# Between the two layers of a graph network kernel: another order, and rooms of their own, for the last three tiles

## What is computed

```
# layer 0
mean = segment_sum(x[src], dst) / max(degree, 1)      # x itself where the degree is 0
x1   = layernorm(x + relu(concat(x, mean) @ W.T + b))
# layer 1: Q, K, V by node type, keys turned by the edge's type
score = sum(Q[dst] * (K[src] @ W_edge[etype])) / sqrt(128) * mu[etype]
out   = segment_sum(softmax_by_dst(score) * V[src])
y     = layernorm(x1 + out)
```

## Time and profile before

| | us |
|---|---|
| median of 3 runs | 2977.58 (2977.36 to 2982.68) |
| the profiled execution | 2978.1 |
| its span, first to last instruction | 2976.3 |
| around the span | 1.8 |
| layer 0, its last gather issued | 928.5 |
| POOL idle between the layers | 928.5 to 969.4 |
| layer 1, from its first gather | 972.9 to 2976.3 |

### The profile page before, as it was taken

How to read it: one execution, slowest core, us unless ns; L and a number is a source line. 1 busy time by engine, 2 the same in 40 slices (tenths; PEclk the granted TensorE clock), 3 DMA queues, 4 the chain that set the end, 5 groups by cost and what they waited for, 6 DMA issues and landing times.

```text
span 2976.3 us, 39076 instructions
## 1 busy us (share of the span) xinstructions
PE 2377.8 (80%) x13828; PEld 1832.4 (62%) x13828; DVE 1543.9 (52%) x5341; ACT 1152.8 (39%) x2071; POOL 2205.6 (74%) x2291
## 2 busy tenths in 40 slices
PE   4999999999998678777777767767767867777776
PEld 2677777777776456556556555655655655655655
DVE  7899999999996233333333333333333333333334
ACT  6565556656564232223233232233222323322223
POOL 7777777777773777777777777777777777777774
PEclk7999999999999688888888888888888888888888
DMA  7355555565554444344444444444434444434442
GB/s 194 104 163 170 160 162 162 162 175 170 164 161 151 119 116 115 112 116 116 114 116 116 112 116 117 115 114 116 115 113 116 116 114 116 116 112 116 115 114 70
DMA packets 256965, 384.07 MB, mean 129 GB/s; under 512 B 100640, under 2 KB 189003, under 8 KB 250625
## 3 DMA queue, kind: packets, MB, share of 16 engines
q0 software_dynamic: 108112, 273.13, 33.1%
q1 hardware_dynamic: 146833, 107.53, 11.7%
q10 hardware_dynamic: 1824, 0.92, 0.1%
HBM read 304.30 MB, written 77.13 MB: 128 GB/s over the span
## 4 chain that ended last, share of the span: by engine, by line
POOL 72%; issue 23%; PE 3%; DMA 1%; DVE 1%; ACT 0%; POOLq 0%; ACTq 0%; DVEq 0%; SPq 0%
POOL ring L722 50%; POOL ring L717 14%; POOL spare_n L717 7%; POOL ring L692 1%; PE banks L789 1%; DMA ring<-in_x_dram 0%; PE banks L1041 0%; PE banks L862 0%; PE banks L1004 0%; PE banks L815 0%; PE banks L867 0%; PE banks L1033 0%; DMA ring<-x_part_rows,work 0%; PE banks L874 0%; DMA x_part_rows<-sums 0%
## 5 line engine op out<-in xcount | busy, mean ns | idle before, releaser
L722 POOL DMA_INDIRECT ring<-kv_table,src_n x1563 | 1495.2, 957 | 476.1 <-issue 476.1
L1017 PE MATMUL banks<-identf,ring 128*128 128x128 f32 x1568 | 293.3, 349 | 505.6 <-DMA ring<-kv_table,src_n 504.4
L1724 DVE COPY sums<-banks 128x512 f32<-128x512 f32 x392 | 260.0, 688 | 738.1 <-PE banks L1033 736.6
L789 PE MATMUL banks<-sums,picks 128*126 128x385 bf16 x2401 | 581.8, 327 | 0.0
L1017 PEld LDWEIGHTS banks<-identf,ring 128*128 128x128 f32 x1568 | 242.2, 182 | 528.6 <-DMA ring<-kv_table,src_n 527.1
L1180 ACT ACTIVATE picks<-banks 128x343 bf16<-128x343 f32 x882 | 433.4, 512 | 317.4 <-PE banks L781 308.5
L717 POOL DMA_INDIRECT ring<-x_part_rows,work x462 | 450.9, 976 | 141.6 <-issue 140.5
L1261 ACT ACTIVATE work<-banks,negmax 128x2048 f32<-128x2048 f32 x98 | 192.8, 1967 | 789.6 <-DVE negmax L1670 775.9
L1269 ACT ACTIVATE work<-banks 128x512 f32<-128x512 f32 x392 | 223.0, 596 | 591.6 <-PE banks L1017 578.4
L1667 DVE TENSOR_REDUCE largest<-banks 128x1 f32<-128x2048 f32 x98 | 224.6, 2292 | 358.4 <-PE banks L1004 358.4
L789 PEld LDWEIGHTS banks<-sums,picks 128*126 128x126 bf16 x2401 | 323.6, 137 | 110.3 <-issue 25.0
(11 more groups left out here) (256 smaller groups left out, 2279.4 us busy)
## 6 DMA issues: line engine op xcount, KB each, us to landing
kv_table<-ring SPq DMA_DIRECT2D x48, 1024.0 KB, 4.1
ring<-kv_table,src_n POOLq DMA_INDIRECT x1563
sums<-x_typed SPq DMA_DIRECT2D x99, 128.0 KB
x_typed<-work SPq DMA_DIRECT2D x49, 256.0 KB
ring<-x_part_rows,work POOLq DMA_INDIRECT x462
x_part_rows<-sums SPq DMA_DIRECT2D x7, 675.5 KB, 5.0
spare_n<-x_part_rows,work POOLq DMA_INDIRECT x224
sums<-x_rows SPq DMA_DIRECT2D x51, 64.0 KB, 3.1
```

The costliest lines, as they stand in the source:

```text
L722: pool.indirect_dma_start(kv_ring[u][:, j, :], None, table, bass.IndirectOffsetOnAxis(ap=of, axis=0)).then_inc(l1_rows[2 * u + j // RUN], 16)
L789: mm = pe.matmul(bank[2 + i % 2][0:SLOTS, 0:3 * D + 1], picked[:, i % 2, h, 0:SLOTS], x_parts[:, h, 0:3 * D + 1], start=(h == 0), stop=(h ...
L1017: tr = pe.transpose(bank[KEY_BANK[g]][:, j * P:(j + 1) * P], kv_ring[k.u][:, g * 4 + j, 0:D], identf[:, :])
L1724: dve.tensor_copy(prob[:, g * 4:(g + 1) * 4, :].rearrange("p a b -> p (a b)"), bank[PROB_BANK[g]]).then_inc(prob_copied, 1)
```

## The change

The last three tiles are called `third` (46), `before` (47) and `last` (48).

- Tile 46's first half is done at the beginning of step 48 (h = 4, 11, 15 in place of 30, 36, 42), in bank 1, and its x1 is turned at h = 34. Tile 47's x and mean are turned at h = 36 and 47, in bank 3. ACT and DVE have an order of their own for this step (`last_step`).
- After the step PE's order interleaves the second halves of the three tiles with the first halves of 47 and 48, as written out below; ACT's and DVE's orders go with it.
- Rooms: the table rows of tile 47 go to `kv_before` and the typed rows of tile 48 to `typed_last`, both in the half of `picks` that step 48 doesn't use. Products of keys go to bank 1 for tile 47 and bank 2 for tile 48, values of tile 48 and the last node sum to bank 4. The turned x1 of all three goes to the fourth quarter of its front bank instead of bank 6.
- Waits are moved with it: those that guarded the shared banks go or move to `low_keys` and `high_keys`, `project_values` of tiles 46 and 47 waits for the copy of the values before (bank 5), and `by_types` of tile 48 no longer waits for the typed rows of tile 47 to be stored.

The diff, cut to its core (left out are the replaced names in the two stores of SP, in `transpose_mean` and `add_nodes`, and the removed PE functions `finish_and_begin` and `late_part`):

```diff
@@ -207,6 +207,9 @@
 near = [t.bitcast(BF16).rearrange("p (j c) -> p j c", c=TW) for t in near_runs]
+late_part = parts(picks, [TILES * P // 2], TILES * P)
+kv_before = late_part(ET * 2 * D).rearrange("p (e c) -> p e c", c=2 * D)
+typed_last = by_type(late_part(NT * D))
@@ -439,10 +442,13 @@
 def kv_of(tile):
-    return kv_last if tile.t == TILES - 1 else kv_rows
+    return {TILES - 1: kv_last, TILES - 2: kv_before}.get(tile.t, kv_rows)
+
+def typed_of(tile):
+    return typed_last if tile.t == TILES - 1 else x1_typedT
...
 def wait_row(e, tile):
-    if 0 < tile.t < TILES - 1:
+    if 0 < tile.t < TILES - 2:
@@ -454,10 +460,24 @@
-FRONT_BANK = {TILES - 1: 0, TILES - 2: 4}
+FRONT_BANK = {TILES - 1: 0, TILES - 2: 3, TILES - 3: 1}
+KEY_PRODUCT = {TILES - 1: 2, TILES - 2: 1}
+VALUE_PRODUCT = {TILES - 1: 4}
...
     return bank[FRONT_BANK[tile.t] if tile.t in FRONT_BANK else 5]
+
+def turned(tile):
+    return front(tile)[:, 3 * P:4 * P] if tile.t in FRONT_BANK else bank[6][:, 0:P]
+
+def key_product(tile):
+    return bank[KEY_PRODUCT.get(tile.t, 7)][:, 0:P]
+
+def value_product(tile):
+    return bank[VALUE_PRODUCT.get(tile.t, 5)][:, 0:P]
+
+def node_sums(i):
+    return bank[4 if i == ND - 1 else 7]
@@ -798,10 +818,9 @@
         if i == ND - 1:
-            wait_nodes(i)
-            pe.wait_ge(kw_high, i - 1)
+            pe.wait_ge(runs_vec, 3 * ND)
         for o in range(2):
-            mm = pe.matmul(bank[7][:, o * (D + 1):(o + 1) * (D + 1)], slot_hot[i % 2][0:SLOTS, o * P:(o + 1) * P],
+            mm = pe.matmul(node_sums(i)[:, o * (D + 1):(o + 1) * (D + 1)], slot_hot[i % 2][0:SLOTS, o * P:(o + 1) * P],
@@ -818,10 +837,6 @@
         pe.wait_ge(x_loaded[tile.k], (tile.turn + 1) * 16)
-        if tile.t == TILES - 1:
-            pe.wait_ge(picked_ready, ND * GCOLS + 2)
-        elif tile.t == TILES - 2:
-            pe.wait_ge(runs_vec, 3 * ND)
@@ -849,31 +864,34 @@
         pe.wait_ge(x1_ready, tile.t + 1)
-        if tile.t >= TILES - 3:
-            wait_low_copied(tile)
-        pe.transpose(bank[6][:, 0:P], x1_tile[tile.k], identf[:, :]).then_inc(x1T_ps, 1)
-
-    def project_keys(tile, sums):
+        pe.transpose(turned(tile), x1_tile[tile.k], identf[:, :]).then_inc(x1T_ps, 1)
+
+    def project_keys(tile):
         pe.wait_ge(typedT_ready, tile.t + 1)
-        if tile.t >= TILES - 3:
-            pe.wait_ge(acc_added, sums)
+        if tile.t == TILES - 3:
...
         for t in range(NT):
-            mm = pe.matmul(bank[7][:, 0:P], wk_s[:, t, :], x1_typedT[:, t, :], start=(t == 0), stop=(t == NT - 1))
+            mm = pe.matmul(key_product(tile), wk_s[:, t, :], typed_of(tile)[:, t, :], start=(t == 0), stop=(t == NT - 1))
...
     def project_values(tile):
+        if TILES - 3 <= tile.t < TILES - 1:
+            pe.wait_ge(v_spread, tile.t + 1)
         for t in range(NT):
-            mm = pe.matmul(bank[5][:, 0:P], x1_typedT[:, t, :], wv_s[:, t, :], start=(t == 0), stop=(t == NT - 1))
+            mm = pe.matmul(value_product(tile), typed_of(tile)[:, t, :], wv_s[:, t, :], start=(t == 0), stop=(t == NT - 1))
...
             pe.wait_ge(weights_ready, ET)
+        if tile.t >= TILES - 3:
+            wait_low_copied(tile)
...
     def high_keys(tile):
+        if tile.t >= TILES - 2:
+            wait_high_copied(tile)
@@ -892,7 +910,7 @@
                 if h == 16:
-                    project_keys(late, added(i))
+                    project_keys(late)
@@ -901,13 +919,26 @@
                 run_sum(i, 1)
-            if early:
+            if early and i + 1 < ND:
...
                     first_product(early)
+            if i + 1 == ND:
+                if h == 4:
+                    transpose_x(early)
+                if h == 11:
+                    transpose_mean(early)
+                if h == 15:
+                    first_product(early)
+                if h == 34:
+                    transpose_typed(early)
+                if h == 36:
+                    transpose_x(tile(TILES - 2))
+                if h == 47:
+                    transpose_mean(tile(TILES - 2))
@@ -922,9 +953,9 @@
                 pe.wait_ge(belongs_ready, 2 * i + 2)
-            if early and h == 29:
+            if early and i + 1 < ND and h == 29:
                 pe.wait_ge(v_spread, early.t + 1)
-            if early and h == 34:
+            if early and i + 1 < ND and h == 34:
@@ -971,12 +986,26 @@
     sweep(l0)
-    transpose_x(tile(TILES - 2))
+    third, before, last = tile(TILES - 3), tile(TILES - 2), tile(TILES - 1)
+    project_keys(third)
+    first_product(before)
+    project_values(third)
     node_sum(ND - 1)
-    finish_and_begin(tile(TILES - 3), tile(TILES - 2))
-    transpose_x(tile(TILES - 1))
-    finish_and_begin(tile(TILES - 2), tile(TILES - 1))
-    late_part(tile(TILES - 1))
+    transpose_x(last)
+    low_keys(third)
+    transpose_typed(before)
+    transpose_mean(last)
+    high_keys(third)
+    first_product(last)
+    project_keys(before)
+    project_values(before)
+    transpose_typed(last)
+    low_keys(before)
+    high_keys(before)
+    project_keys(last)
+    project_values(last)
+    low_keys(last)
+    high_keys(last)
@@ -1194,24 +1223,35 @@
         act.wait_ge(k_ps, tile.t + 1)
-        act.activation(kT, bank[7][:, 0:P], ACT.Copy).then_inc(kT_ready, 1)
+        act.activation(kT, key_product(tile), ACT.Copy).then_inc(kT_ready, 1)
...
         wait_row(act, tile)
-        act.activation(kv_of(tile)[:, :, D:2 * D], bank[5][:, 0:P].unsqueeze(1).broadcast_to([P, ET, D]), ACT.Copy
+        act.activation(kv_of(tile)[:, :, D:2 * D], value_product(tile).unsqueeze(1).broadcast_to([P, ET, D]), ACT.Copy
...
+    def last_step(late, early):
+        copy_x(early)
+        copy_mean(early)
+        copy_key(late)
+        deviation(early)
+        copy_projected(late)
+        copy_high(late)
+        copy_x(tile(TILES - 2))
+        copy_mean(tile(TILES - 2))
+
     def l0(i, late, early):
+        if i + 1 == ND:
+            return last_step(late, early)
         for c in range(GCOLS):
-            if i + 1 < ND:
-                if c == 0:
-                    act.wait_ge(slots_ps, i + 2)
-                take(i + 1, c, (i + 1) % 2)
+            if c == 0:
+                act.wait_ge(slots_ps, i + 2)
+            take(i + 1, c, (i + 1) % 2)
@@ -1225,19 +1265,7 @@
-    def late_part(tile):
-        copy_key(tile)
-        copy_projected(tile)
-        copy_high(tile)
-
     act.sem_inc(v_spread, 1)
-
-    def finish_and_begin(old, new):
-        copy_mean(new)
-        copy_key(old)
-        copy_projected(old)
-        deviation(new)
-        copy_high(old)
@@ -1245,11 +1273,20 @@
     sweep(l0)
-    copy_x(tile(TILES - 2))
-    finish_and_begin(tile(TILES - 3), tile(TILES - 2))
-    copy_x(tile(TILES - 1))
-    finish_and_begin(tile(TILES - 2), tile(TILES - 1))
-    late_part(tile(TILES - 1))
+    third, before, last = tile(TILES - 3), tile(TILES - 2), tile(TILES - 1)
+    copy_key(third)
+    deviation(before)
+    copy_x(last)
+    copy_projected(third)
+    copy_mean(last)
+    copy_high(third)
+    copy_key(before)
+    deviation(last)
+    copy_projected(before)
+    copy_high(before)
+    copy_key(last)
+    copy_projected(last)
+    copy_high(last)
@@ -1500,11 +1537,11 @@
         dve.wait_ge(types_loaded[tile.k], (tile.turn + 1) * 16)
-        if tile.t > 0:
+        if 0 < tile.t < TILES - 1:
...
         for t in range(NT):
-            ins = dve.scalar_tensor_tensor(x1_typedT[:, t, :], ntype_rows[tile.k], float(t), bank[6][:, 0:P],
+            ins = dve.scalar_tensor_tensor(typed_of(tile)[:, t, :], ntype_rows[tile.k], float(t), turned(tile),
@@ -1553,7 +1590,24 @@
+    def last_step(i, late, early):
+        before = tile(TILES - 2)
+        normalise_x1(late)
+        join_parts(i - 1, (i - 1) % 2)
+        mean(early, added(i) - 1)
+        add_nodes(i - 1)
+        by_types(late)
+        relu(early)
+        normalise_x1(early)
+        add_runs(i)
+        copy_low(late)
+        mean(before, added(i + 1) - 1)
+        by_types(early)
+        place_slots(i)
+
     def l0(i, late, early):
+        if i + 1 == ND:
+            return last_step(i, late, early)
@@ -1592,8 +1646,6 @@
             hot(i + 2, i % 2, 1)
-        if i == ND - 1:
-            normalise_x1(early)
@@ -1619,19 +1671,17 @@
     join_parts(ND - 1, (ND - 1) % 2)
-    before, last = tile(TILES - 2), tile(TILES - 1)
-    mean(before, added(ND) - 1)
+    third, before, last = tile(TILES - 3), tile(TILES - 2), tile(TILES - 1)
+    relu(before)
     add_nodes(ND - 1)
-    by_types(tile(TILES - 3))
-    relu(before)
-    copy_low(tile(TILES - 3))
...
     by_types(before)
+    copy_low(third)
     relu(last)
-    copy_low(before)
...
     by_types(last)
+    copy_low(before)
```

(22 more changed lines are left out.)

## The result

| | before | changed |
|---|---|---|
| median of 15 runs each, us | 2979.26 (2977.36 to 2984.91) | 2972.54 (2969.24 to 2974.74) |
| ratio | 1 | 0.9975, 95% [0.9968, 0.9982] |
| profiled execution | 2978.1 | 2972.4 |
| its span | 2976.3 | 2970.6 |
| last slot product begins | 939.4 | 940.0 |

The change saves 7.4 us by the ratio (5.4 to 9.5), and 6.7 between the two medians; the forecast was 9.65. In the two profiled executions the first gather comes 9.3 us earlier, and the end 5.7.

A forecast was written before the change was run, and what follows sets the result against it. POOL's gathers bound the kernel, starting after a 40.9 us idle between layers. PE's ladder ends 10.45 us earlier, backlog leaves 9.65 at the last landing, tail 0: 2977.58 becomes 2967.9, range 2965.0 to 2972.5.

The forecast's parts named there:

- What bounds the kernel: Second layer: POOL alone paces 1563 gathers at 1.261 us; a microsecond won in its preceding 40.9 us idle shortens the end.
- PE's work behind the slot products: Between the layers: 12.56 us of PE work after 940.04, plus waits and 0.3, ending high_keys(48) at 954.3 against 964.75.
- The waits: PE after the last step: 1.0 us at transpose_mean(48) and 0.35 at x1(48), together 1.38 us.
- The added load behind table 45: Tile 48's x, queued behind table 45, lands by 942.0, wanted 942.8; 1 us late would be mostly absorbed by the next wait.
- The backlog: Stores of tables 47 and 48 run back to back on DMA; last landing at 959.0 instead of 968.63, 9.65 us.
- The other estimate: DMA stores between layers: bytes over 436 GB/s gives 5.5 us for 2.4 MB, almost no backlog, gain 10.4 us.
- The rival of the clock that falls once more: Between layers: PE's clock falls at 945, costing about 3.1 us; gain 6.6, time 2971.0; chance 0.15.
- The low clock's price: PE between layers: slow keys, values, low keys and product of tiles 46 and 47 cost 4.2 us and a little more.
- The tail: Behind the last gathers: PE's low-clock loss may shift with the clock's phase, between -2.1 and +1.4 us; taken as 0.
- The base: Whole kernel before: median 2977.58 us, from which the forecast was taken; the profiled run lies 0.5 above it.
- The signs of being wrong: Low clock 941 to 954; DMA-released transpose_x(48) gap; landing over 4 us after issue; gathers above 1.261 us; tail over 33.3.
- The rooms: New buffers for the last tiles: cost no instruction; removed waits were on conditions long met or on these buffers.

The follow-up runs named there:

- early_undone: Changed kernel with tile 46's front and the early transposes of tiles 46 and 47 put back; last slot product to first gather 28.3 and 28.4 us, second run's ratio 0.9998.
- Before_filled: Kernel before with identity transposes added in PE's waits between the layers; 2980.39 us, ratio 0.9997 to before.
- Tail_fill: Changed kernel with forty identity transposes on PE ahead of the keys of the block before the last; 2973.86 us, ratio 0.9975 to before.
- before_third: Kernel before, unedited, traced a third time on a chip where it takes about 3600 us; last slot product to first gather 30.6 us.

## Why the prediction was right, and where a term was off

The forecast was 2967.9, in a range of 2965.0 to 2972.5; the median is 2972.54, 0.04 above the range's upper end and 4.6 above the forecast. The ratio, put on the three runs' median of 2977.58 that the forecast stood on, gives 2970.1. So the forecast range was missed by a hair by the median and held by the ratio; the mechanism was right, and the size of the gain was off. By its steps:

- **What bounds the kernel**: right. The first gather moved by 9.3 us, layer 1 kept its 1970 us (1969.7 to 1970.9 in the four later traces on a 2981-us chip, 1973.0 in the one that the result shows), and the medians moved by 6.7 and 7.9 us.
- **PE's work behind the slot products**: they end at 940.37 (forecast 940.04). From there to the end of high_keys(48) it is 14.11 us, without 1.17 of waits 12.94 of work; forecast were 12.56 and 0.3 in proportion. The waits were to be 1.38 and were 1.17, at partly other places: 1.0 had been put at transpose_mean(48), where 0.25 was found, because transpose_x(48) had already waited 0.54 for its load. The end of high_keys(48) was forecast at 954.3 and came at 954.48.
- **The added load behind table 45**: SP issued it at 938.46, 0.85 us behind table 45, and PE could use it at 943.58, not by 942.0: 0.54 us of wait, which the next wait mostly absorbed, as the prediction said that it would. So this small load took up to 5.1 us behind the table's 1 MB. The Trainium skill (DMA: Bandwidth & Descriptors, "Queues, rings and completion order") says that a DMA engine takes the descriptors of a ring in order; the 5.1 us agree with that, though no row shows the descriptors themselves.
- **The backlog**: the last landing was to come at 959.0 and came at 959.34, 4.21 us after its issue instead of 3.23. Table 47 stored in halves took 0.7 us off (halves_47), as a backlog would have it. The other estimate, by the fit in the Trainium skill (DMA: Bandwidth & Descriptors, "Anatomy of one DMA"), had nearly no backlog and a gain of 10.4; the landing moved by 9.3, so it is contradicted. The page gives that fit for DMAs issued by GpSimd, and these are issued by SP.
- **The clock between the layers**: it stays at 1.00 in all three traces of this order on the fast chip. The rival of the clock that falls once more didn't come true here, though in early_undone, with 2.1 us more of waits, it did in both runs.
- **The low clock's price: the term that was mis-sized.** The sum priced the removed falls at about 4.2 us and a little more, from the only trace there was. Before_filled gives 4.2 for that trace, so the price was right for it. But the other two traces of before lose less: the clock falls once and is back sooner, and against the one on the same chip as before_filled the same removal gives 1.6. Against that trace the change shortens POOL's idle stretch by 38.4 − 31.2 = 7.2 us, the tail takes 0.6 back, and 6.6 is left; the medians differ by 6.7 and 7.9. How often before has one fall and how often two isn't known from three traces.
- **The tail**: taken as 0 between −2.1 and +1.4; it was 0.6 longer in both traces of the change (33.9 against 33.3 in two traces of before). The low clock's loss in it isn't the same each time: the 16 probability transposes took 3.00 and 3.17 in the two traces of before, 3.41 in both of the change. But in every trace without the tail fill the whole tail lay between 33.0 and 34.7, so no run shows it swing between the prediction's ends. The Trainium skill (TensorE: Matmul & The Clock Gate, "What's actually happening") says that the stretch over which PE's activity is judged runs freely; these differences agree with that and don't prove it. Tail_fill shows that the lower end, −2.1, couldn't be had: with the clock full the tail is 32.6, 0.7 less than before's 33.3.
- **The base**: the prediction stood on three runs with a median of 2977.58. Fifteen runs give 2979.26, and 22 later ones 2980.99. So 1.7 of the 4.6 us are the base, and the other 2.9 are the gain (9.65 forecast, 6.7 between the medians): about 0.6 the tail, 0.4 the first gather (9.3 for 9.65), and the remaining 1.9 fits the low clock of which two of three traces of before have less. This last share is argued from the traces, not counted in the timed runs.
- **The signs of being wrong**: four of those named appeared, all small. The wait at transpose_x(48) was ended by a DMA (0.54 us), the last landing came over 4 us after its issue (4.21), the tail was over 33.3 us (33.9), and the gathers of the first trace were slower than 1.261 us (1973.0 us for the 1562 steps from the first to the last, 1.263 each). The fifth, a low clock from 941 to 954, didn't.
- **The rooms** had been costed at no instruction and no gain of their own. The runs show that the order depends on one of them: without typed_last a wait is back at another place, and 2.1 us of the 5.6 of the order are lost where the clock stays full, up to 3.1 where it falls in that wait.

## What to carry to other kernels

The ladder of short dependent steps between the two layers paid twice here, in its waits and in the clock that fell behind them. Three tiles interleaved so that each fills the other's waits took 9.8 us out of 33.5 in one pair of traces and 7.3 out of 30.9 in another, and the fill alone (extra work in the waits) shows how much of it is the clock. Look at a second trace before a clock's fall is priced: instruction durations at full clock and PE's waits ahead of tile 46 came back in each, the second fall did not. And give the last tile its own buffers when its work is drawn forward, or a store's landing takes the place of the wait that was removed.

## What of the hardware was not expected

- **The same waits, different falls.** With the same instructions, and the same waits of PE (1.75, 0.30 and 0.73 us) ahead of the keys of tile 46, the clock fell in all three traces of before. But it stayed low until the low keys of tile 46 in the first and only until its values in the others, and fell a second time only in the first. Together that makes 2.6 to 2.9 us of ladder. With 2.2 us of idle PE ahead of the same keys of tile 48 it fell in two of three.
- **Layer 0 varies nearly as much as the change is worth.** Its last slot product begins between 939.4 and 946.1 us in six traces, and goes with the time of the same 686 gathers on POOL: 669.1 us busy in the earliest trace, 675.1 in the latest, 975 against 984 ns each. (Before_filled is the exception: its first slot product comes 2.7 us later than in the first trace.) Two traces are therefore compared from a mark inside the program, not from the span's start.
- **A chip on which the same program takes 3600 us.** Waits of POOL in before_third (engine, line, releaser: us in total, times, longest):
```profile
POOL ring L722 <- remote: 294.9, 94, 3.4
POOL ring L717 <- PE banks L815: 216.1, 61, 9.1
```
POOL waits 94 times, about 3 us each, for something that the profile only calls remote, and in layer 0 for PE, which the traces of before on the faster chip don't show. A gather there still takes 961 ns and keys at full clock 0.89 to 1.16 us. What these waits are was not found. An edit whose effect lies in one stretch can still be read from such a trace; its whole time can't.
